# Four graph layers on one Trainium2 core: in the second layer's gather, SyncE fetches 16 of 2048 rows

## The reference, cut to what matters

```python
x = fea @ Wlin.T + blin                    # then batch norm over the nodes, leaky ReLU
h = x @ Wg.T
deg = segment_sum(ones_like(dst), dst, n);  dinv = where(deg > 0, rsqrt(deg), 0)
msgs = (dinv[src] * dinv[dst])[:, None] * h[src]
out = segment_sum(msgs, dst, n) + bg       # then log_softmax
```

## Time and profile before

| | |
|---|---|
| timed runs | 12719.03 and 12743.06 us, median 12731.05 us |
| profiled execution | 12712.1 us, span 12710.4 us |
| second layer's gather stretch | 3662 to 6045 us of the span, 101 rounds |
| GpSimd there | 1616 gathers of 0.946 us, 1528.3 us busy |
| TensorE there | 1549.4 us busy of 2383.0, granted clock 0.50 |
| DMA engines there | 21% busy, 53 GB/s |

### The profile page before, as it was taken

One profiled execution on the slowest core, in us unless ns is written; L12 is line 12 of the kernel. 1 busy time (PEld: TensorE's weight loads), 2 busy tenths in 40 slices (PEclk: granted clock), 3 DMA queues, 4 the chain that ended last, 5 costly groups with the idle time before them and its releaser, 6 DMA issues. The chain is left out here.

```text
span 12710.4 us, 135705 instructions
## 1 busy us (share of the span) xinstructions
PE 6918.1 (54%) x31117; PEld 5819.8 (46%) x31117; DVE 5032.6 (40%) x11110; ACT 1829.1 (14%) x2950; POOL 6152.5 (48%) x6479
## 2 busy tenths in 40 slices
PE   4555455555346666666444444444443576776764
PEld 4444444444346565656133333434342454554543
DVE  4333333333532222222334454545445343333334
ACT  0000000000110000000100000000001344444443
POOL 4444444444136666666034545455440366666662
PEclk6555665555555555555556666666665667677776
DMA  4222222222112222222033333333330122222221
GB/s 122 69 70 70 69 71 70 69 70 70 24 37 53 53 53 53 53 53 53 17 100 110 112 110 114 111 110 113 109 96 1 51 57 57 58 58 57 57 57 38
DMA packets 621338, 882.10 MB, mean 69 GB/s; under 512 B 305955, under 2 KB 413142, under 8 KB 621294
## 3 DMA queue, kind: packets, MB, share of 16 engines
q0 software_dynamic: 232704, 536.56, 16.0%
q1 hardware_dynamic: 372894, 334.04, 8.8%
q10 hardware_dynamic: 15696, 11.01, 0.3%
HBM read 848.63 MB, written 32.40 MB: 69 GB/s over the span
## 5 line engine op out<-in xcount | busy, mean ns | idle before, releaser
L1447 POOL DMA_INDIRECT PM<-hgt_kv_table,TMP x1616 | 1531.8, 948 | 1910.7 <-PE ps L1479 1035.2
L591 POOL DMA_INDIRECT PM<-gat_table,TMP x1616 | 1528.9, 946 | 1753.2 <-PE ps L630 1220.7
L1941 POOL DMA_INDIRECT TMP<-schnet_table,TMP x1616 | 1561.1, 966 | 1500.6 <-DVE PM L2015 523.0
L1110 POOL DMA_INDIRECT TMP<-gcn_table,TMP x1616 | 1528.3, 946 | 1227.6 <-issue 461.2
L1125 PE MATMUL ps<-rows,PM 16*128 16x8 f32 x3232 | 756.0, 359 | 739.6 <-DVE PM L1166 601.7
L1125 PEld LDWEIGHTS ps<-rows,PM 16*128 16x128 f32 x3232 | 717.7, 323 | 841.7 <-DVE PM L1166 643.3
L1132 PE MATMUL ps<-TMP 128*128 128x128 f32 x3232 | 838.1, 441 | 103.8 <-DVE TMP L1160 87.7
L1968 PE MATMUL ps<-PM 128*128 128x128 f32 x3232 | 629.7, 358 | 472.8 <-DVE PM L2018 434.4
L1968 PEld LDWEIGHTS ps<-PM 128*128 128x128 f32 x3232 | 583.3, 270 | 496.9 <-issue 454.3
L609 PE MATMUL ps<-PM 128*128 128x4 f32 x3232 | 745.2, 354 | 92.7 <-DMA PM<-gat_table 40.0
L1132 PEld LDWEIGHTS ps<-TMP 128*128 128x128 f32 x3232 | 719.3, 327 | 116.1 <-issue 88.5
(11 more groups left out here) (350 smaller groups left out, 9956.6 us busy)
## 6 DMA issues: line engine op xcount, KB each, us to landing
PM<-local_dst_row SPq DMA_DIRECT2D x404, 512.0 KB
PM<-in_attrT SPq DMA_DIRECT2D x404, 100.0 KB
PM<-gat_table,TMP POOLq DMA_INDIRECT x1616
TMP<-gcn_table,TMP POOLq DMA_INDIRECT x1616
PM<-hgt_kv_table,TMP POOLq DMA_INDIRECT x1616
TMP<-schnet_table,TMP POOLq DMA_INDIRECT x1616
TMP<-in_src_et SPq DMA_DIRECT2D x808, 2.0 KB
PM<-in_rel_row SPq DMA_DIRECT2D x202, 64.0 KB
```

The source lines that it names most:

```text
L591: pool.indirect_dma_start(out=g[:, par, t, 0:ROW0], out_offset=None, in_=tab0_d, in_offset=bass.IndirectOffsetOnAxis(ap=idx[:, par, t:t + ...
L1110: pool.indirect_dma_start(out=g[:, b, k, :], out_offset=None, in_=tab1_d, in_offset=bass.IndirectOffsetOnAxis(ap=idx[:, b, k:k + 1], axis= ...
L1447: pool.indirect_dma_start(out=g[:, par, t, 0:2 * P], out_offset=None, in_=kv_d, in_offset=bass.IndirectOffsetOnAxis(ap=idx[:, par, t:t + 1 ...
L1941: pool.indirect_dma_start(out=g[:, b, k, :], out_offset=None, in_=tab3_d, in_offset=bass.IndirectOffsetOnAxis(ap=idx[:, b, k:k + 1], axis= ...
```

## The change

SyncE gets a new step, `fetch_rows`, at the head of each round of its loop, and once more after the loop for the last round. It waits for the indices of group 3 and for all sums of the round before. Then, for each of the partitions 112 to 127, it reads the index of tile 3 of group 3 from SBUF into a register and issues a transfer of one table row (512 bytes) into that partition of `g`. GpSimd's sixteenth gather of a round covers 112 rows instead of 128; the other fifteen are as before. TensorE waits for the 16 transfers ahead of group 3's sums.

```diff
+SP_ROWS = 16
@@ gather stretch of the second layer
+        row_gath = sem("gcn_rows_gathered")
+        LAST = P - SP_ROWS
@@ SyncE
+                def fetch_rows(i):
+                    sp.wait_ge(idx_ready[SLOTS - 1], 16 * (i + 1))
+                    sp.wait_ge(agg, i * SLOTS + SLOTS)
+                    for p in range(LAST, P):
+                        met(sp)
+                        r = sp.value_load(idx[p:p + 1, SLOTS - 1, KT - 1:KT], min_val=0, max_val=NP - 1)
+                        sp.dma_start(g[p:p + 1, SLOTS - 1, KT - 1, :], tab1_d[bass.ds(r, 1), :]).then_inc(row_gath, 16)
+
                 with sp.Fori(0, NR - 1) as i:
+                    fetch_rows(i)
                     for b in range(SLOTS):
                         sp.wait_ge(gath[b], 16 * KT * (i + 1))
                         met(sp)
...
+                fetch_rows(NR - 1)
@@ GpSimd
                         for k in range(KT):
+                            n = LAST if b * KT + k == ROUND - 1 else P
                             pool.indirect_dma_start(
-                                out=g[:, b, k, :], out_offset=None, in_=tab1_d,
-                                in_offset=bass.IndirectOffsetOnAxis(ap=idx[:, b, k:k + 1], axis=0)).then_inc(gath[b], 16)
+                                out=g[0:n, b, k, :], out_offset=None, in_=tab1_d,
+                                in_offset=bass.IndirectOffsetOnAxis(ap=idx[0:n, b, k:k + 1], axis=0)).then_inc(gath[b], 16)
@@ TensorE
                             pe.wait_ge(gath[b], 16 * KT * (i + 1))
+                            if b == SLOTS - 1:
+                                pe.wait_ge(row_gath, 16 * SP_ROWS * (i + 1))
```

## The result

| | before | changed |
|---|---|---|
| timed runs | 12719.03 and 12743.06 us, median 12731.05 | 14221.44 and 14228.46 us, median 14224.95 |
| profiled execution, span | 12712.1, 12710.4 us | 14221.44, 14219.7 us |
| a round of the gather stretch | 23.59 us | 38.44 us |

The changed kernel takes 1.1176 times as long (95% interval 1.1149 to 1.1203), 1,494 us more. The forecast was 14,460 us with a range of 13,750 to 15,100.

The account below looks back on a forecast made before the run. The round was taken as GpSimd's 19.7 us of gathers plus a 3.8 us hand-over. With 24.6 us slow part plus 16.2 us of rows, 17.2 us more over 101 rounds gave 14,460 us, range 13,750 to 15,100.

Parts of the forecast that it names:

- The mechanism: In the second layer's gather stretch, gathers and SyncE's rows come one after the other; 17.2 us more a round, chance 0.79.
- The slow part, 24.6 us: From a row step's end: 2.0 us lead to the first gather, gathers to 21.7, SyncE slow until 24.6 us.
- SyncE's other five loads ... 10 to 19 us: Loads between row steps, mostly at 0.80 us an instruction; next row step at T + 12 to T + 20.
- T: The end of a row step, SyncE's issue of a round's 16 rows; the forecast counts the round's times from it.
- The round's sums are complete at T + 4.9.: On TensorE: last row lands at T + 2.8, group 3's sums take 2.1 us, beside the gathers and free.
- A quick row, 1.16 us: SyncE's price for one row while GpSimd is idle; 14 such rows a round make 16.2 us.
- only part of the slow phase counts: Rival: six or seven rows fit beside the gathers; a round of 35.6 us, 13,940 us, inside the range; no separate chance.
- Removed from GpSimd: nothing.: The sixteenth gather covers 112 rows; at best 0.16 us a round or 16 us in all, taken as nothing.
- Added on TensorE: one wait, costs the arrival.: One wait a round ahead of group 3's sums, costing only the rows' arrival, which lies beside the gathers.
- Every row is slow: Rival: SyncE's rows stay at 5.6 us even with GpSimd idle; a period of about 95 us, 19,900 us, chance 0.04.
- 2 us when quiet: Rival: a row costs SyncE about 2 us with GpSimd idle; a round of 54.6 us, 15,870 us, chance 0.07.
- SyncE keeps its quick pace: Rival: gathers do not slow SyncE; 16 rows take 18.6 us, the chain 23.5 us, about 12,740 us, chance 0.09.

Follow-up runs that it names:

- half_gathers: The changed kernel with every second of GpSimd's gathers left out and the others counted double; 13356.7 us, ratio 1.0478 against the kernel before.
- rows8_again: The changed kernel with 8 rows a round by SyncE instead of 16, on a chip with slow SyncE; 13220.61 us, ratio 1.0377 against the kernel before.
- spread: The changed kernel with SyncE's 16 rows split into four per group, each with its own wait and semaphore; 13502.46 us, ratio 1.0361 against the kernel before.
- rows_late: The changed kernel with the row step moved behind the first three index loads and the types; 13558.36 us, ratio 1.0642 against the kernel before.
- rows0: The changed kernel with its waits but no rows fetched by SyncE, run on two chips; 9548.08 and 13008.79 us, ratios 1.0001 and 0.9993.
- quarter_products: The changed kernel with three of four TensorE products of the gather stretch left out; 14547.49 us, ratio 1.1172 against the kernel before.
- rows20: The changed kernel with 20 rows a round by SyncE instead of 16, on the quick chip; 10561.02 us, ratio 1.1064 against the kernel before.

## Why the prediction was right, and where its sizes were off

**The mechanism stands.** Forecast: gathers with the slow phase first, then rows, GpSimd idle for about 20 us for want of indices. Measured: 18.95 and 19.48 us, ended by the index load. Half of the gathers (half_gathers) takes 8.7 us off the round, and half of the rows (rows8_again) takes 10.1 off, eight times the quick pace. That the slow phase follows the gathers is shown by its length; what makes it is not shown.

**The slow part, 24.6 us.** Measured 26.0 in the mean: lead 2.9 instead of 2.0, gathers 19.8, tail 3.3 instead of 2.9. This is +1.4 us.

**"SyncE's other five loads ... 10 to 19 us": this step failed.** I priced them by the slow phase, as if it began with the gathers. All six were quick: from 4546.85 to 4550.48, 3.6 us, and over by T + 4.0. The next row step then began at T + 4.9, with its first transfer at T + 5.9, and not at T + 12 to T + 20. The slow phase set in only 3 to 4 us after the first gather. So it took in six rows at some 3.5 us each instead of two at 5.6: four quick rows fewer, -4.6 us.

**"The round's sums are complete at T + 4.9."** The number is the start of the row step, but by luck. The sums were complete at T + 3.1; the step waited for SyncE's own loads and for the last of them to land (T + 4.4). The experiments spread and rows_late were planned on the chain through the sums, which ends no wait of SyncE in the changed kernel.

**A quick row, 1.16 us.** It is 1.25: the transfer is cheaper to issue than I took (0.255 instead of 0.34), the register load dearer (0.44 instead of 0.27). 10.1 x 0.09 = +0.9 us. Together +1.4 - 4.6 + 0.9 = -2.3 us a round, or about 235 of the 14,460 us forecast. The forecast came out nearer than its largest error, because the two others cancel half of it; that is luck. The working's case "only part of the slow phase counts" (13,940) had the number of rows right, six or seven, and came out too low by the slow part and the price of a quick row.

On the register load the Trainium skill's floor of about 600 ns (DMA: Bandwidth & Descriptors, Latency and other measured facts) is again above what the trace has, 0.438 to 0.459 us in the quick rows. The measurement decides.

**"Removed from GpSimd: nothing."** Right in both rows0 runs. A gather of 112 rows takes 0.93 us, one of 128 rows 0.945.

**"Added on TensorE: one wait, costs the arrival."** Right: TensorE's 1,377 us behind row transfers lie beside GpSimd's idleness, and quarter_products shows that the amount of its work does not bound.

**The rivals.** "Every row is slow" and "2 us when quiet" are refuted by the quick rows (1.25). "SyncE keeps its quick pace" is wrong on the chip measured, but describes the chip of rows20; its chance of 0.09 was given for the wrong reason, as I put it down to places in the code. Even there 16 rows would not be free, since a row is 1.25 us and the chain 25.0 us, against a round of 20.05.

**What stays open.** What the slow phase is; whether the gathers' instructions or their transfers bring it; why one chip has none; why it sets in late in the changed kernel and was nearly absent beside the second half of the gathers in rows_late; and what holds TensorE's counts back in it.

## What to carry to other kernels

Before you give work to a queue that looks idle, ask what stands behind that work in its order: here six loads for the next round, the first of which starts GpSimd. A queue that is late by its own work delays every engine whose inputs it issues, and the price is that of its slowest phase plus the remainder at its quick pace. Putting the rows behind three of the four index loads gave back 6.4 of 14.85 us here. Look for what gets an index into a register before you look at the transfers: taking it out gave back 13.2 us. Taking an eighth off one of 16 gathers saves nothing, since a gather of 112 rows takes nearly as long as one of 128 (0.93 and 0.945 us). And ask on which chip a number was taken: one chip ran the kernel before in 9,547 us and did without the slow phase.

## What the runs showed of the hardware that was not expected

- While GpSimd gathers, SyncE moves in steps of about 0.7 us where the kernel before takes 12,731 to 13,016 us: an instruction, register arithmetic included, takes 0.70 us or next to nothing (0.005 us), and a row 3.5 us in the mean instead of 1.25. On the chip where the kernel before takes 9,547 us none of the 2,020 register loads takes over 0.482 us, none of line 1096's register operations over 0.167 (rows20). The granted clock of the gather stretch is 0.50 in both cases, so TensorE's clock is not the difference.
- The slow phase begins 3 to 4 us after the first gather in the changed kernel and ends 3.3 us after the last one (mean; 1.9 us with half of the gathers). In the kernel before it can begin sooner: in the round of the earlier trace rows SyncE's loop branch at 4559.75, 1.3 us after the first gather, takes 0.67 us.
- TensorE's semaphore counts come late in the same phase, if it has much to do. ScalarE starts over 1 us after the product that it waits for in 243 of 404 cases in the kernel before, in none in rows0 on the quick chip, and in none in quarter_products.
- The length of a gather's instruction is no straight function of its rows: 0.93 us for 112, 0.98 for 108 and 120, 1.29 for 124, 0.945 for 128.
- A register load from an index tile at partitions 112 to 127 takes 0.44 us, one from `first_i` 0.27. Why was not tried.
